# One memory sum for the mixture: all experts' rows added onto x2, and eight block loads in the last pass

## The reference

```python
x = _layernorm(x + self_attention(x))
x = _layernorm(x + cross_attention(x, ctx))        # this x is "x2" in the kernel
# mixture: 8 routed experts, 2 per token, capacity 1280 rows each; 2 shared experts for every token
logits = x @ gate_w.T; scores = softmax(logits)
topk_w, topk_idx = top_k(scores, 2); topk_w = topk_w / (topk_w.sum(-1) + 1e-20) * keep
y  = sum over a token's kept experts of comb * (silu(x @ we_gate.T) * (x @ we_up.T)) @ we_down.T
sh = silu(x @ ws_gate.T) * (x @ ws_up.T) @ ws_down.T   # both shared experts
x  = _layernorm(x + y + sh)
```

## Time and profile before

| | us |
|---|---|
| median of 3 runs | 1431.15 (1428.96 to 1433.54) |
| the profiled execution | 1442.53 |
| its span | 1440.8 |
| attention | to 1021.8 |
| jobs 0 to 9 | 1021.8 to 1171 |
| 40 routed chunks | 1171 to 1363 |
| last pass | 1363 to 1440.8 |

### The profile page before, as it was taken

The page is one execution under the profiler, slowest core; times in us unless marked ns, Lnnn a source line. Parts: engine busy times, 40 slices in busy tenths (PEclk is TensorE's granted clock), DMA queues, the critical chain, the costliest instruction groups (busy, mean ns, idle before and its releaser), DMA issues. The chain is left out here.

```text
span 1440.8 us, 27468 instructions
## 1 busy us (share of the span) xinstructions
PE 1336.4 (93%) x8424; PEld 812.1 (56%) x8424; DVE 1088.6 (76%) x2228; ACT 920.5 (64%) x1763; POOL 465.4 (32%) x484
## 2 busy tenths in 40 slices
PE   3999999999999999999999999999698999999984
PEld 2434454444444445444454444434687889999964
DVE  5889889888978978987998888895466545555476
ACT  3387767776677776776767777686354445655544
POOL 3334204202401510330250201021155436666753
PEclk8799999999999999999999999999688799999997
DMA  6544444243334424433434442330354347786752
GB/s 172 139 145 137 141 126 131 82 147 117 119 119 129 138 70 142 141 90 133 129 118 123 126 135 84 113 99 16 108 186 163 107 121 133 134 171 134 153 179 88
DMA packets 109946, 181.48 MB, mean 126 GB/s; under 512 B 20352, under 2 KB 67584, under 8 KB 105728
## 3 DMA queue, kind: packets, MB, share of 16 engines
q1 hardware_dynamic: 94656, 159.90, 35.5%
q0 software_dynamic: 14592, 19.41, 7.6%
q10 hardware_dynamic: 576, 0.79, 0.4%
HBM read 99.67 MB, written 79.30 MB: 124 GB/s over the span
## 5 line engine op out<-in xcount | busy, mean ns | idle before, releaser
L833 DVE TENSOR_REDUCE nm<-ps_ring 128x1 f32<-128x512 f32 x1024 | 638.9, 680 | 52.8 <-PE ps_ring L1035 52.2
L790 ACT ACTIVATE prob<-ps_sc 128x512 f32<-128x512 f32 x1024 | 551.5, 600 | 195.7 <-PE ps_sc L1050 194.5
L1035 PE MATMUL ps_ring<-qk 48*128 48x512 f32 x1024 | 408.4, 472 | 13.7 <-DMA qk<-hbm_self 7.5
L1050 PE MATMUL ps_sc<-qk 50*128 50x512 f32 x1024 | 389.9, 454 | 10.9 <-ACT prob L790 9.9
L1050 PEld LDWEIGHTS ps_sc<-qk 50*128 50x128 f32 x1024 | 161.3, 187 | 300.8 <-ACT prob L790 215.6
L1067 PE MATMUL ps_out<-prob,va 128*32 128x512 f32 x2048 | 275.6, 610 | 1.6 <-ACT ot L669 0.7
L1817 PE MATMUL ps_gu<-x2f,we 128*128 128x256 f32 (+1 forms) x1344 | 221.1, 320 | 3.7 <-ACT sg L1488 2.4
L1817 PEld LDWEIGHTS ps_gu<-x2f,we 128*128 128x128 f32 x1344 | 190.1, 192 | 19.8 <-DVE h L1708 2.8
L1035 PEld LDWEIGHTS ps_ring<-qk 48*128 48x128 f32 x1024 | 167.1, 189 | 44.9 <-DVE nm L833 27.0
L1817 PE MATMUL ps_dn<-we,hf 128*128 128x256 f32 x864 | 125.2, 304 | 11.5 <-DVE totals L1791 10.3
L1817 PEld LDWEIGHTS ps_dn<-we,hf 128*128 128x128 f32 x864 | 119.4, 213 | 13.3 <-DVE hf L1712 12.1
(11 more groups left out here) (168 smaller groups left out, 1617.3 us busy)
## 6 DMA issues: line engine op xcount, KB each, us to landing
qk<-hbm_cross SPq DMA_DIRECT2D x384, 64.0 KB, 2.3
qk<-hbm_self SPq DMA_DIRECT2D x372, 64.0 KB, 2.3
hbm_self<-stage SPq DMA_DIRECT2D x16, 1024.0 KB, 3.9
hbm_cross<-stage SPq DMA_DIRECT2D x16, 1024.0 KB, 4.1
slots_x<-zeros SPq DMA_DIRECT2D x8, 1360.0 KB, 5.9
xs<-slots_x SPq DMA_DIRECT2D x40, 272.0 KB
weraw<-w_moe SPq DMA_DIRECT2D x11, 768.0 KB, 4.3
x2in<-x SPq DMA_DIRECT2D x16, 512.0 KB, 4.5
```

The costliest lines, as they stand in the source:

```text
L790: nc.scalar.activation(prob[:, s % 2, j, :], ps_sc[:, score_bank(h.cur, HG * s + j), :], ACT.Exp, scale=HD ** -0.5).then_inc(exp_done[a], 1)
L833: nc.vector.tensor_reduce(nm[:, g % 2, r:r + 1], bank(slot), axis=AX.X, op=ALU.max, negate=True).then_inc(max_done[a], 1)
L1035: nc.tensor.matmul(bank(slot), qk[rows, 0, pair, P * c:P * c + P], qk[rows, 1, pair, :], start=True, stop=True).then_inc(smax_done[a], 1)
L1050: nc.tensor.matmul(ps_sc[:, score_bank(inst, n), :], qk[rows, 1, h // 2, P * c:P * c + P], qk[rows, 0, h // 2, :], start=True, stop=True). ...
```

## The change

- `sums` is gone. `x2` takes every addition.
- The first shared expert's block is no longer stored by SP but added onto `x2` by POOL, in one adding DMA of 128 x 4 rows of 256 values (`add_shared(i)`). It stands on POOL behind the scatters of block i + 1, and waits for `ym_done` of job i and for the same kind of DMA two jobs earlier.
- All experts add onto `x2`. At each expert's first chunk from expert 1 on, POOL waits for all adds of the expert just before.
- The last pass loads 8 blocks of `x2` straight into `totals`, all after the last adds, each with a semaphore of its own. POOL's `both` and the second buffer's turn-taking go.
- Attention clears the spare rows of one tensor instead of two.

```diff
-                        for rows in spare_rows:
-                            sp.dma_start(rows[h.clear, :, :, :],
-                                         zeros[0:SPARE_P, 0:D].unsqueeze(1).to_broadcast([SPARE_P, SPARE_A, D])) \
-                                .then_inc(cleared, 16)
+                        sp.dma_start(spare_rows[h.clear, :, :, :],
+                                     zeros[0:SPARE_P, 0:D].unsqueeze(1).to_broadcast([SPARE_P, SPARE_A, D])) \
+                            .then_inc(cleared, 16)
...
             for i in range(B):
-                sp.wait_ge(ym_done, out_of_job(i, 1))
-                sp.dma_start(even_rows[i], ym[:, i % MARGIN, :, :]).then_inc(sums_out[i % 2], 16)
...
-            for c in range(NCH):
-                sp.wait_ge(added[c], 16 * CT * (NE - 1))
-            sp.wait_ge(dn_done, of_chunk(CHUNKS - NCH - 1))
-            for n in range(6):
-                load_even(n)
             for c in range(NCH):
                 sp.wait_ge(added[c], 16 * CT * NE)
-            for n in range(HELD):
-                load_odd(n)
-            for n in range(6, B):
-                load_even(n)
-
             for n in range(B):
-                if n + HELD < B:
-                    sp.wait_ge(both_done, n + 1)
-                    load_odd(n + HELD)
+                sp.dma_start(total(n), x2_rows[JOBS[B + n][0]]).then_inc(sum_in[n], 16)
+
+            for n in range(B):
...
+            def add_shared(i):
+
+                if i >= 2:
+                    pool.wait_ge(sums_out[i % 2], 16 * (i // 2))
+                pool.wait_ge(ym_done, out_of_job(i, 1))
+                nc.gpsimd.dma_start(x2_rows[i], ym[:, i % MARGIN, :, :], accum_op=ALU.add).then_inc(sums_out[i % 2], 16)
...
+                if i:
+                    add_shared(i - 1)
+            add_shared(B - 1)
...
-                if c == 0 and is_chunk(g - 2 * NCH):
+                if c == 0 and is_chunk(g - NCH):
 
                     for n in range(NCH):
-                        wait_alone(pool, added[n], 16 * CT * (e - 1), consts, 9)
+                        wait_alone(pool, added[n], 16 * CT * e, consts, 9)
...
-                        x2 if j // NCH else sums, bass.IndirectOffsetOnAxis(ap=dest[:, c, t:t + 1], axis=0),
+                        x2, bass.IndirectOffsetOnAxis(ap=dest[:, c, t:t + 1], axis=0),
...
-            def both(n):
-                pool.wait_ge(even_in[n // 3], 16 * (2 if n // 3 == 2 else 3))
-                pool.wait_ge(odd_in[n % HELD], 16 * (n // HELD + 1))
-                nc.gpsimd.tensor_tensor(total(n), total(n), xin[:, n % HELD, :, 0:D], ALU.add).then_inc(both_done, 1)
...
             def moments(n):
                 q = n % 2
-                dve.wait_ge(both_done, n + 1)
+                dve.wait_ge(sum_in[n], 16)
```

More of the change, by code:

```diff
@@ L285, in wait_alone, with attention_phase @@
     eng.wait_ge(s, value)
-def attention_phase(nc, x, xT, cT, w_att, tables, b_cols, bo_rows, x2, hbm_self, hbm_cross, slots_x, sums,
+def attention_phase(nc, x, xT, cT, w_att, tables, b_cols, bo_rows, x2, hbm_self, hbm_cross, slots_x,
                     w_first, x2_out, rooms):
@@ L451, in stacked @@
                         sp.wait_ge(stack_in[a][g], b * 192)
-            spare_rows = [rows[B * T:, :].rearrange("(k p a) d -> k p a d", k=B, p=SPARE_P) for rows in (sums, x2)]
+            spare_rows = x2[B * T:, :].rearrange("(k p a) d -> k p a d", k=B, p=SPARE_P)
             shares = slots_x.rearrange("g p t d -> (g p t) d").rearrange("(k p a) d -> k p a d", k=B, p=P)
@@ L539, in _ @@
             sp.wait_ge(x2_out, (B - 1) * 16)
[L540 removed]
+            sp.wait_ge(cleared, 2 * B * 16)
         @block.gpsimd
@@ L1151, in rooms_ahead, with moe_phase @@
         return [ctx.enter_context(nc.sbuf_tensor(name, [P] + ROOMS[name], F32 if name == "weraw" else F32R)) for name in ROOMS]
-def moe_phase(nc, x2, slots_x, sums, w_moe, w_gate, index, numbers, out, x2_out, rooms):
+def moe_phase(nc, x2, slots_x, w_moe, w_gate, index, numbers, out, x2_out, rooms):
     with ExitStack() as ctx:
@@ L1236, in moe_phase @@
         added = [sem(f"added{c}") for c in range(NCH)]
-        even_in = [sem(f"even_in{s}") for s in range(3)]
-        odd_in = [sem(f"odd_in{n}") for n in range(HELD)]
-        both_done, total_done, moments_done, rstd_done, norm_done = (
-            sem("both_done"), sem("total_done"), sem("moments_done"), sem("rstd2d"), sem("norm_done"))
+        sum_in = [sem(f"sum_in{n}") for n in range(B)]
+        total_done, moments_done, rstd_done, norm_done = (
+            sem("total_done"), sem("moments_done"), sem("rstd2d"), sem("norm_done"))
         out_done = sem("out_done")
@@ L1298, in split_next @@
             return n, par, (kk + 1 if par else kk + 2) + 1
-        even_rows = sums[0:TOKENS, :].rearrange("(i t p) d -> i p t d", t=TT, p=P)
-        odd_rows = x2[0:TOKENS, :].rearrange("(i t p) d -> i p t d", t=TT, p=P)
+        x2_rows = x2[0:TOKENS, :].rearrange("(i t p) d -> i p t d", t=TT, p=P)
         @block.sync
@@ L1434, in _ @@
             by_pairs(pool, CHUNKS, add, NCH)
-            def both(n):
-                pool.wait_ge(even_in[n // 3], 16 * (2 if n // 3 == 2 else 3))
-                pool.wait_ge(odd_in[n % HELD], 16 * (n // HELD + 1))
-                nc.gpsimd.tensor_tensor(total(n), total(n), xin[:, n % HELD, :, 0:D], ALU.add).then_inc(both_done, 1)
-            for n in range(2):
-                both(n)
             for n in range(B):
                 q = n % 2
-                if n + 2 < B:
-                    both(n + 2)
                 pool.wait_ge(moments_done, 2 * TT * (n + 1))
@@ L1963 @@
 SCRATCH = {"x2": [TOKENS + CAP, D], "hbm_self": [FC, P, SLOTS, T], "hbm_cross": [FC, P, SLOTS, T],
-           "slots_x": [CHUNKS, P, CT, ROW], "sums": [TOKENS + CAP, D]}
+           "slots_x": [CHUNKS, P, CT, ROW]}
 def program(nc, ap, scratch, out):
```

11 lines of the change are left out of this document (3 added, 8 removed).

## The result

The changed kernel takes 1435.82 us in the median of 20 runs, against 1428.35 for the kernel before (20 runs). The ratio is 1.005, with a 95% interval of 1.0035 to 1.0065: it is slower by about 7 us. A second measurement beside other kernels gave 1.0052 [1.0023, 1.0081]. One of the 20 runs took 2295.11 us and is left out of the ratio; without it the median is 1435.47. The forecast was 1425.2, range 1420.5 to 1433.0.

A forecast was written before the change was run, and what follows sets the result against it. The prediction took PE to bound the routed chunks and DVE, held by POOL's wide additions, the last pass. Its terms, -7.2 + 1.2 = -6.0 us, taken from the median, gave 1425.2 us, range 1420.5 to 1433.0.

The forecast's parts named there:

- the last pass: Last pass: without POOL's wide additions DVE's beat falls from 8.73 and 7.09 to 5.70 us, 7.2 us less.
- rival C: Last pass: with smaller gaps PE keeps its higher clock, 2.2 us more are won, 1423.0; chance 0.13.
- rival D: Last pass: L1786 is slow by itself with two operands in SBUF, so DVE is not freed, 1432.4; chance 0.07.
- POOL's price for `add_shared`: First stage: one 512-row adding instruction costs POOL between 1.55 and 7.1 us, taken as about 4, adding nothing.
- rival A: First stage: POOL pays by row, 6.2 us or more per `add_shared`, last scatter late, 1426.7 up to 1432.1; chance 0.20.
- a POOL instruction of up to 5.7 us is covered: First stage: POOL waits 36.3 us before scatters of blocks 2 to 7, 6.05 each, so such an instruction costs nothing.
- mostly outside the stages concerned: Whole kernel: where the profiled execution's 11.4 us above the median lay, so the same 6.0 us was subtracted from the median.
- the load of chunk 0: Start of the routed stage: two 512 KB adding DMAs beside this load delay it by 1.2 us, bounds 0 to 4.3.
- the new wait: Each expert's first chunk: POOL's wait for the adds just before costs nothing, as those adds land in time.
- Rival B: Expert boundaries: adds land late, deciding from landing time L = 4.4; at 5.8 us 17 us lost, 1442; chance 0.10.
- the weight load falls on an expert's second chunk: Routed chunks: argument against late-landing adds, that this load does not meet an expert's last and first chunks.
- The 2.1 us of lateness: Routed chunks: DVE's pick once waited 2.11 us for adds without PE idling, so about that much lateness is free.

The follow-up runs named there:

- both parts undone: Changed kernel with two tensors, SP's stores and the wait of before again, so only its last pass is left; 0.9956 to the kernel before.
- the later execution of before: A second traced execution of the unchanged kernel before, run as a kernel of its own; 1424.02 us, ratio of that run 1.0013.
- the late load: Complete changed kernel with each expert's weight load issued two chunks later; 1.0014 to the kernel before.
- both mends: Complete changed kernel with weight loads two chunks later and the last two shared adds issued after chunks 0 to 3 landed; 0.9963, then 1.0015.
- last two adds held back: Changed kernel with the shared adds of blocks 6 and 7 issued only once chunks 0 to 3 have landed; 1.0029 to the kernel before.
- the third execution of before: A third traced execution of the unchanged kernel before, within 1 us of its median; 1427.42 us.

## Why the prediction was wrong

**Right: the last pass.** -7.2 forecast, -7 in the traces, -6.3 by the ratio of the kernel with both parts undone, through the mechanism named: DVE freed from POOL's additions. The clock did not come back (rival C), and L1766 was not slow by itself (rival D): in the later execution of before, too, L1786 takes 0.68 us where POOL is not adding, and 2.05 to 2.90 where it is. Data was there in time, though the loads landed later (10.1 us) than the 7.3 allowed for.

**Off, but harmless: POOL's price for `add_shared`.** The forecast took about 4 us between its two ends, and it was 1.45 us, so rival A as it was put did not come. The Trainium skill, "DMA: Bandwidth & Descriptors", section on the anatomy of a DMA on the gpsimd path, stood for the low end, and the trace agrees: 1.45 us for 512 rows.

**Wrong: "a POOL instruction of up to 5.7 us is covered".** That slack of 36.3 us was read from an execution whose first stage was 13 to 16 us longer than usual. In the later one the brackets ahead of blocks 2 to 7 are 4.32, 4.25, 3.52, 3.42, 3.54 and 1.42, together 20.5 us, or 3.4 us each. That still covers 1.45 plus 0.3 everywhere but ahead of block 7, where 0.3 us are lost. With the 4 us that the forecast took it would not have. The prediction saw that this execution was 11.4 us above the median and put the excess "mostly outside the stages concerned"; it lay in the first stage. Subtracting a difference from the median was right; taking the slack of that stage from this execution was not.

**Wrong: what the shared adds do to other transfers.** This is the step that failed first. Their 4.3 us of DMA time each (by the shares of POOL's queue below, some 3.4 is the better estimate) was counted only against the load of chunk 0, with 1.2 us taken between 0 and 4.3. PE's wait there grew by 2.96 us (3.15 to 6.11), and by 0.9 more at the lower clock. The six adds in the stage before were costed by POOL's time alone. Four of them start 1.4 to 3 us ahead of a block load, and block loads land at 5.9 us instead of 3.9; PE waits, and some matmuls behind it run at the lower clock (4.58 instead of about 3 us per 12). The last scatter comes 4 to 7 us later. No term of the sum, and no rival, had this. That late loads are the only way from the adds to the late scatter stays open, as said above.

**Wrong: the new wait.** Rival B named the mechanism with its deciding point (L = 4.4) and got 0.10. Two steps of the term put at nothing failed. L was taken as 2.3 us, from the last adds of all with little beside them; the median of the changed kernel's adds is 4.0. And "the weight load falls on an expert's second chunk" held only while the first chunk's adds were on time. With L = 4.0 the first of them starts 2.7 us later, and the changed kernel's rows show where that puts the second: at 1229.53, with the load at 1230.48; then L is 7.4 to 7.9. The 2.1 us of lateness that the earlier trace rows called free are confirmed: with the late load DVE's longest wait is 2.2 and PE stays busy.

In the sum: -7 as forecast, start of the routed stage and first stage +6 to +9 in place of +1.2, wait +7.4 in place of 0.

## What to carry to other kernels

An extra DMA has three prices: the time of the engine that issues it, its own landing, and what it does to every transfer that starts beside it; list the last for each place where it is issued, also where its own completion is wanted by nobody. A landing time must be taken from rows under the same load as the place in question, and a delay of a few us must be followed to the next large transfer in the program, since it may slide under it. And the slack of a stage is to be read from an execution that is typical of that stage; one that is 1% above the median has its excess somewhere, and the busy time of the same matmuls by stage shows where.

## What the runs showed of the hardware

- An adding DMA of 512 KB on POOL's queue landed after 6.7 us (median of 8), a plain one of the same size and queue after 3.6, and SP's store after 3.7. Beside the adding ones SP's 512 KB loads went from 3.9 to 5.9 us. In the first stage POOL's queue took 39.6% of the 16 DMA engines' time over 130 us with the eight adding DMAs, 28.6% over 130 us with eight plain ones, and 20.5% over 120 us with neither. By these shares an adding DMA of 512 KB takes some 3.4 us of all 16 engines and a plain one 1.6; both are estimates.
- Adding onto SBUF works as well as onto memory: `totals<-x` landed after 6.2 us and took 1.32 us of POOL, both in the median of 8.
- An add (128 rows, indirect) that started 1.0 to 1.7 us ahead of a 768 KB load took 7.43 to 7.86 us to land, against a median of 4.0.
- PE's clock made small waits dear: idle times of 1.95, 2.28 and 3.08 us were followed at once by 12 matmuls of 4.58 to 4.60 us instead of about 3.0; behind 1.39 and 1.56 us they took 2.98. The length of the wait does not decide alone: behind 2.21 us they took 3.01 (last two adds held back), and behind a wait of 1.45 us at the same place of the stage 4.11 in the third execution of before and 2.99 in the later one.
- One chip ran the kernel before in 1446.06 us where others took 1428 to 1430, and in the two traces from it the first mixture stage is 149 to 150 us with 129 to 130 us of busy PE, against 130 to 133 with 118 to 121 for the kernel before elsewhere; there the change with both mends was faster (0.9963) and elsewhere it was not (1.0015).
